# First cross attention of a four-layer block: where the heads are divided, and when TensorE weighs the values

## The chip, the cores and the metric

The program runs on one core of a Trainium2 chip. A core has five engines with an instruction queue each: TensorE (PE in the profile; PEld are its weight loads), VectorE (DVE), ScalarE (ACT), GpSimd (POOL) and SyncE (SP), which here only issues DMAs. They meet at semaphores alone. The metric is the device time of one execution in microseconds.

## What is computed

Four layers follow each other on `x` of 4 batches by 512 rows by 256: a cross attention, an expert attention, a second cross attention and product-key experts. The change is in the first, in its hand-over to the second, and nowhere else:

```python
def _L0_xattn_ref(x, kv, mask, attn_bias, WQ_w, WQ_b, WK_w, WK_b, WV_w, WV_b, WO_w, WO_b):
    B, S, E, H = (2, 512, 256, 16)          # B is 4 here: it is read from x.shape
    DK = E // H
    Q, K, V = ...                           # (x @ W.T + b), 16 heads of 16
    T = jnp.einsum('bhqd,bhkd->bhqk', Q, K) / math.sqrt(DK)
    T = T + attn_bias[:, None, :, :]
    T = jnp.where(m2[:, None, :, :] == 0, -1000000000.0, T)
    A = jax.nn.softmax(T, axis=-1)
    out = jnp.einsum('bhqk,bhkd->bhqd', A, V)
    out = out.transpose(0, 2, 1, 3).reshape(b, sq, E)
    return out @ WO_w.T + WO_b

x = x + tanh(g_xattn[0]) * _L0_xattn_ref(_layernorm(x), ctx_1024, mask, bias, ...)
```

## The kernel before

`a_attention` does the first attention in 64 steps: 4 batches, in each 4 groups of 4 heads, in each 4 tiles of 128 query rows. Step n has batch b = n // 16 and i = n % 16. All five queues are written out by hand, and each engine has a loop over n of its own. Everything is float32. The PSUM banks are SB (four, the scores of a step), TB (two, transposed probabilities), OB (the weighted values of a group) and MB (one, shared by all other jobs).

In step n TensorE does, in this order: `scores(n)` into SB, after VectorE has read the scores of step n-1; `turn_probs(n-1, 0)`, which transposes the probabilities of two of the four heads into TB, after both halves of step n-2 have been copied out of TB; at most one *job* in MB; `turn_probs(n-1, 1)` for the other two heads, into the same TB, after ScalarE has copied the first two out; and `weigh`, half of the value product of a pair of steps, two to three steps late. The jobs are the projections q, k and v (`queries`, `keys`, `values`), the transposes of the next batch's x (`turn_x`), the output projection of the last batch (`outputs`, one tile each) and `inverses`. Where a step has no job, `keep_busy` does one 128x512 matmul that nobody reads, once MB's last job has been taken. `slot(n)` is the table of jobs, and OUT_AT lists the steps of `outputs`. A job may start when the job before it has been taken out of MB (`bank_free`).

VectorE does `lowest` four times in step n: it adds the bias to the scores of a head and takes the least value. Then `take_pair(n-1)` copies TB's second half of step n-1 to SBUF, and then come what jobs it has to take (q, k, `update` of x by an output) and the statistics `stat` of the next batch. ScalarE does `take_pair(n-1)` of the first half, four exponentials (`spread_probs`, each with a row sum read from an accumulator), the jobs v and x, and once in four steps `take_o`, which copies OB to SBUF.

The value tile `vtok` has for each head 16 columns of values and 16 of ones, so that the 32 rows that a head has in OB are 16 of unnormalised output and 16 equal rows of the sum of its probabilities. Before, these sums are not read: VectorE takes reciprocals of the accumulated row sums (`invert`), TensorE spreads them over rows with 16 matmuls (`inverses`), and VectorE multiplies OB's copy by them (`normalise`) into `onorm`. `compact` on SyncE then moves the four heads of a group with four DMAs into `whole`, where a batch's 256 rows lie densely in two tiles, and `outputs` reads `whole`. The last batch's output projection is done within the second layer (`late_output` in `b_attention`), and the move of its last group too.

SyncE's queue also has `move`: eight DMAs each that spread q or k of two groups over strips of 32 partitions, which `scores` read; and `load_bias`. GpSimd has in batch b: `find_root`, `stage_x`, `shift_x` (layer norm of the next batch), `fold_bias` four times (mask and bias of the next batch into `bneg`, which `lowest` reads) and `fold_rows`.

## Time and profile before

| | us |
|---|---|
| median of 3 runs | 2248.33 |
| lowest and highest run | 2246.73, 2257.74 |
| the profiled execution | 2246.41 |
| its span, first to last instruction | 2244.6 |

| the first attention, in the profiled execution | us |
|---|---|
| scores of step 0 start | 19.18 |
| scores of step 16, 32 and 48 start | 101.48, 179.53, 257.58 |
| scores of step 63 start | 328.45 |
| TensorE's first matmul of the second layer | 346.83 |

Of the span, 347 us belong to the first attention, and the change touches nothing behind the first 100 us after it. A row of the timeline below is start, duration, engine, line, operation, out<-in and count; a matmul's own end is modelled and lies some 0.07 us behind the start of the next matmul that follows without a gap, so costs on TensorE are read from start to start. A float32 matmul is recorded as two instructions, a transpose as one.

### The profile page before, as it was taken

What the parts mean: (1) busy time and instruction counts of PE and PEld (TensorE: products, weight loads), DVE (VectorE), ACT (ScalarE), POOL (GpSimd) and SP (SyncE); (2) the same over time, 40 slices, a digit from 0 to 9 for tenths busy, and PEclk for the clock granted to TensorE, in tenths of its full rate; (3) what the DMA queues carried; (4) which work ended last, traced back from release to release, by engine and by line L of the source; (5) the groups of instructions that cost most, each with busy time, mean ns of one, the idle gap of its engine ahead of it and who ended that gap; (6) DMA issues with size and microseconds to landing.
All of it is one profiled execution on the core that took longest, in us unless ns stands there. A gap on an engine that the chain in (4) does not pass through costs nothing. (4 is left out here: it accounts for less than half of the span.)

```text
span 2244.6 us, 45912 instructions
## 1 busy us (share of the span) xinstructions
PE 2172.1 (97%) x18243; PEld 1463.3 (65%) x18276; DVE 1685.6 (75%) x4495; ACT 815.4 (36%) x1943; POOL 178.5 (8%) x427
## 2 busy tenths in 40 slices
PE   7999999999999999998999999999889999999998
PEld 3555554445756756775555555556678989898997
DVE  7888885866566566535887787877698988888895
ACT  4888881311311311302654554545321121111210
POOL 5553201000000000000000000000000000000000
PEclk9999999999999999999999999999999999999999
DMA  5111103000000003001000000001200000000000
GB/s 178 27 39 47 26 10 153 1 1 1 1 1 1 1 0 113 1 1 50 2 1 1 1 1 1 1 1 58 95 1 2 1 11 2 1 11 1 2 11 11
DMA packets 24165, 48.65 MB, mean 22 GB/s; under 512 B 5008, under 2 KB 13456, under 8 KB 22928
## 3 DMA queue, kind: packets, MB, share of 16 engines
q1 hardware_dynamic: 23952, 45.71, 6.1%
q8 instruction: 146, 2.39, 0.4%
q14 instruction: 67, 0.55, 0.1%
HBM read 37.57 MB, written 2.10 MB: 18 GB/s over the span
## 5 line engine op out<-in xcount | busy, mean ns | idle before, releaser
L2286 PE MATMUL banks<-work,big 128*128 128x128 f32 x2048 | 252.7, 277 | 2.0 <-PEq L376 1.3
L2286 PEld LDWEIGHTS banks<-work,big 128*128 128x128 f32 x2048 | 246.2, 193 | 7.6 <-issue 3.2
L614 ACT ACTIVATE work<-banks,work 128x512 f32<-128x512 f32 x256 | 174.8, 687 | 203.9 <-DVE work L731 203.9
L1085 PE MATMUL banks<-big,work 128*128 128x256 f32 x1024 | 241.3, 379 | 3.6 <-issue 3.3
L1009 PE MATMUL banks<-big,work 128*128 128x512 f32 x512 | 228.4, 600 | 1.6 <-DMA big<-in_B_val 1.4
L2379 ACT ACTIVATE work<-banks 128x512 f32<-128x512 f32 x128 | 76.5, 598 | 408.6 <-PE banks L2286 405.3
L1085 PEld LDWEIGHTS banks<-big,work 128*128 128x128 f32 x1024 | 195.0, 190 | 33.9 <-issue 1.9
L1904 ACT ACTIVATE work<-work 128x512 f32<-128x512 f32 x256 | 181.0, 711 | 0.0
L1009 PEld LDWEIGHTS banks<-big,work 128*128 128x128 f32 x512 | 96.0, 191 | 116.0 <-issue 113.3
L731 DVE TENSOR_REDUCE work<-banks 128x2 f32<-128x1024 f32 x128 | 150.4, 1217 | 7.7 <-PE banks L470 7.7
L1307 DVE CUSTOM_DVE_ANT_0 work<-banks,work 128x512 f32<-128x512 f32 (+3 forms) x128 | 57.7, 488 | 121.5 <-PE banks L1025 109.2
L1276 DVE TENSOR_TENSOR work<-banks,work 128x512 f32<-128x512 f32 x128 | 88.1, 691 | 65.7 <-PE banks L1009 65.4
L1808 PEld LDWEIGHTS banks<-ident,work 64*128 64x128 f32 x2048 | 75.5, 139 | 90.2 <-ACT work L1904 58.7
L1192 ACT ACTIVATE work<-work 128x512 f32<-128x512 f32 (+3 forms) x128 | 70.8, 554 | 168.7 <-DVE work L1307 168.6
L484 PEld LDWEIGHTS banks<-ident,work 64*128 64x128 f32 x2048 | 74.0, 139 | 89.1 <-issue 51.5
L2313 PE MATMUL banks<-big,wab 128*128 128x256 f32 x512 | 125.3, 388 | 3.5 <-DVE wab L2524 3.5
L470 PE MATMUL banks<-work 64*128 64x256 f32 x1024 | 124.6, 383 | 0.9 <-DVE work L724 0.9
L2313 PE MATMUL banks<-big,work 128*128 128x256 f32 x512 | 123.7, 387 | 0.8 <-DVE work L2524 0.8
L497 PE MATMUL banks<-big,wc 128*64 128x512 f32 x512 | 116.9, 598 | 5.2 <-ACT wc L635 2.9
L749 DVE COPY big<-banks 128x512 f32<-128x512 f32 x128 | 87.6, 684 | 38.9 <-PE banks L484 38.7
L740 DVE TENSOR_SCALAR work<-work 128x512 f32<-128x512 f32 x256 | 113.0, 484 | 4.5
L2303 PEld LDWEIGHTS banks<-wc 128*128 128x128 bf16 x3072 | 106.6, 98 | 13.3 <-issue 5.1
(248 smaller groups left out, 3791.7 us busy)
## 6 DMA issues: line engine op xcount, KB each, us to landing
work<-work SPq DMA_DIRECT2D x152, 32.0 KB, 2.0
big<-in_bias SPq DMA_DIRECT2D x16, 256.0 KB, 4.6
big<-in_B_val SPq DMA_DIRECT2D x8, 512.0 KB, 7.0
big<-in_B_out SPq DMA_DIRECT2D x1, 4096.0 KB, 18.9
big<-in_D_downT SPq DMA_DIRECT2D x4, 1024.0 KB, 5.5
big<-in_D_up SPq DMA_DIRECT2D x1, 4096.0 KB, 15.4
wc<-in_ctxT SPq DMA_DIRECT2D x1, 2048.0 KB, 7.8
wab<-in_L_ffn_w_q SPq DMA_DIRECT2D x1, 2048.0 KB, 10.1
```

The source lines that it names most:

```text
L470: last = eng.matmul(SB[i][:, j, c * 256:(c + 1) * 256], qT[r, t % 2, qt * P:(qt + 1) * P], kT[r, t % 2, c * 256:(c + 1) * 256], start=True ...
L497: last = eng.matmul(FB[0][j * DK:(j + 1) * DK, :], vtok[:, kt, h * DK:(h + 1) * DK], pT[:, (t % 2 * PAIR + j) * QT + kt, :], start=(kt == ...
L614: eng.activation(prob[:, n % NS * PAIR + j, :], SB[n % 2][:, j, :], ACT.Exp, bias=low[:, n % NS, j:j + 1], accum_out=rowsum[:, n % NS, j:j ...
L731: eng.tensor_reduce(low[:, n % NS, :], SB[n % 2], AX.X, ALU.max, negate=True).then_inc(low_ready.sem, 1)
L740: last = eng.tensor_scalar(one, one, rinv[:, n % NS, j:j + 1], None, ALU.mult)
L1009: last = eng.matmul(value_bank(b, n), xnT[:, kc, t * P:(t + 1) * P], w_val[:, kc, h * EB * DK:(h + 1) * EB * DK], start=(kc == 0), stop=(k ...
L1085: last = eng.matmul(XO[qt // 2][:, qt % 2 * D:(qt % 2 + 1) * D], spread[:, c % NG, qt * P:(qt + 1) * P], w_out[:, c, :], start=False, stop ...
L1276: eng.tensor_tensor(scaled[:, n % NG, :].rearrange("p (k e) -> p k e", e=EB), value_bank(b, n).rearrange("p (k e) -> p k e", e=EB), gm[:, ...
L1904: eng.activation(one, one, ACT.Exp, bias=low[:, n % 2, j:j + 1], scale=-1.0, accum_out=rowsum[:, n // QT % 2, at:at + 1]).then_inc(p_ready, 1)
L2286: last = eng.matmul(HP[n % 2][:, q * P:(q + 1) * P], down[:, (n * NJ + q) * KC + kc, :], xnT[par][:, kc, :], start=(kc == 0), stop=(kc == ...
L2303: last = eng.matmul(dst, hot[:, c, at, :], lot[c][:, at, f, :], start=(f == 0), stop=(f == 2))
L2313: last = eng.matmul(UPP[par][:, 0:D], G[par][:, j, :], up[:, j, :], start=(j == 0), stop=(j == ELO - 1))
```

## The change

- **Division.** `invert`, `inverses`, `normalise` and the row sums of the exponentials go. `take_o` copies OB, heads and sums, into one of two tiles. `gather_heads` on SyncE replaces `compact`: four DMAs move the rows of sums of a group into `sums`, four more the undivided heads into `whole`. `weigh_heads` on GpSimd then, for each *pair* of groups (one dense tile of 128 rows), finds 1/sums with a seed and three Newton steps and multiplies the tile: 11 instructions of 128x512. There are eight pairs; pair 2b and 2b+1 are the halves of batch b. `sums` is one tile, so a gather of the next pair waits until the pair before has been weighed (`weighted`). `outputs` waits for `weighted` instead of the moves.
- **Where GpSimd weighs.** Pair 2b-2 after the bias of batch b has been folded, pair 2b-3 ahead of `find_root(b)`, the last pair in the second layer.
- **Order on TensorE.** `weigh` stands between the two halves of `turn_probs`, behind the job, and no longer after the second.
- **Padding.** The unread matmuls of the steps without a job go. The loops end one step sooner.
- **Jobs** move: k to i = 2 and 4, v to 6, outputs to 8, 9, 12 and 15, x to 10 and 11.

```diff
-    OUT_AT = (5, 6, 10, 12)
+    OUT_AT = (8, 9, 12, 15)
...
+def gather_heads(eng, m, heads, whole, sums, g):
+    A = A_
+    for j in range(A.group):
+        r, at = (g % 2 * A.group + j) * A.dk, A.strip * j + A.dk
+        eng.dma_start(sums[r:r + A.dk, :], heads[at:at + A.dk, :]).then_inc(m["A.sums_moved"][g % 2], 16)
+    for j in range(A.group):
+        r, at = (g % 2 * A.group + j) * A.dk, A.strip * j
+        eng.dma_start(whole[r:r + A.dk, g // 2, :], heads[at:at + A.dk, :]).then_inc(m["A.compacted"][g], 16)
...
+def weigh_heads(eng, m, pair, whole, sums, inverse, product, step):
...
+    eng.tensor_scalar(inverse.bitcast(I32), sums.bitcast(I32), -1.0, INVERSE_SEED, ALU.mult, ALU.add).then_inc(step, 1)
+    for k in range(NEWTON):
...
+        eng.tensor_tensor(product, inverse, sums, ALU.mult).then_inc(step, 1)
...
+        eng.tensor_scalar(product, product, -1.0, 2.0, ALU.mult, ALU.add).then_inc(step, 1)
...
+        eng.tensor_tensor(inverse, inverse, product, ALU.mult).then_inc(step, 1)
...
+    eng.tensor_tensor(whole[:, kc, :], whole[:, kc, :], inverse, ALU.mult).then_inc(m["A.weighted"], 1)
...
+                def gather(b, g):
+                    eng.wait_ge(o_taken, G * b + g + 1)
                     if b >= 2:
                         eng.wait_ge(job_made, MADE[("out", b - 2, QT - 1)])
+                    eng.wait_ge(weighted, (G * b + g) // 2)
+                    gather_heads(eng, m, oT[g % 2], whole[b % 2], sums, g)
...
                 for b in range(1, B):
+                    if b >= 2:
+                        eng.wait_ge(row_step, ROWS * (b + 1))
+                        weigh_heads(eng, m, 2 * b - 3, whole[b % 2], sums, mm, bt, m["A.newton_step"])
                     find_root(eng, b)
                     stage_x(b)
...
+                    eng.wait_ge(fold_step, fold_at(b, QT - 1))
+                    weigh_heads(eng, m, 2 * b - 2, whole[(b - 1) % 2], sums, mm, bt, m["A.newton_step"])
...
                     if t == 0:
-                        for g in range(G):
-                            eng.wait_ge(compacted[g], 16 * GH * (b + 1))
+                        eng.wait_ge(weighted, 2 * b + 2)
...
-                    if 5 < n <= LAST and slot(n) is None:
-                        sem_, count = took([slot(k) for k in range(n) if slot(k) is not None][-1])
-                        eng.wait_ge(sem_, count)
-                        keep_busy(MB, 1)
+                    if n >= 3 and (n - 3) // 2 < LAST // 2:
+                        weigh((n - 3) // 2, (n - 3) % 2)
                     if 1 <= n <= LAST:
                         turn_probs(n - 1, 1)
-                    if n >= 3 and (n - 3) // 2 < LAST // 2:
-                        weigh((n - 3) // 2, (n - 3) % 2)
...
-                    eng.activation(one, one, ACT.Exp, bias=low[:, n % 2, j:j + 1], scale=-1.0,
-                                   accum_out=rowsum[:, n // QT % 2, at:at + 1]).then_inc(p_ready, 1)
+                    eng.activation(one, one, ACT.Exp, bias=low[:, n % 2, j:j + 1], scale=-1.0).then_inc(p_ready, 1)
```

How the queues change at two places. TensorE's queue in batch 1, steps i = 6 and 7, before: scores (L1794), a half of the transposes (L1808), the job (L1774 is `outputs`, L1762 `inverses`), the other half, `weigh` (L1824).

```order
L1794 MATMUL banks<-work 128x512 x4
L1808 MATMUL banks<-ident,work 128x64 x16
L1774 MATMUL banks<-wab,big 128x256 x2
L1808 MATMUL banks<-ident,work 128x64 x16
L1824 MATMUL banks<-wc,big 32x256 x8
L1794 MATMUL banks<-work 128x512 x4
L1808 MATMUL banks<-ident,work 128x64 x16
L1762 MATMUL banks<-ident,work 32x128 x16
L1808 MATMUL banks<-ident,work 128x64 x16
L1824 MATMUL banks<-wc,big 32x256 x8
```

The same steps of the changed kernel, where L1782 is `values`, L1852 `weigh`, L1836 the halves and L1822 the scores:

```order
L1822 MATMUL banks<-work 128x512 x4
L1836 MATMUL banks<-ident,work 128x64 x16
L1782 MATMUL banks<-wab,big 128x256 x4
L1852 MATMUL banks<-wc,big 32x256 x8
L1836 MATMUL banks<-ident,work 128x64 x16
L1822 MATMUL banks<-work 128x512 x4
L1836 MATMUL banks<-ident,work 128x64 x16
L1852 MATMUL banks<-wc,big 32x256 x8
L1836 MATMUL banks<-ident,work 128x64 x16
```

The second half of the transposes is now the last thing ahead of the next scores, and between its end and the next first half only the scores are left.

SyncE's queue from batch 1's second half into batch 2, before: L1589 is `compact`, L1579 `move`, L1567 the bias loads.

```order
L1589 DMA work<-work 16x512 [waits A_dve_took]
L1589 DMA work<-work 16x512 x3
L1579 DMA work<-work 16x512 [waits A_scores_made,A_dve_took]
L1579 DMA work<-work 16x512 x7
L1579 DMA work<-work 16x512 [waits A_scores_made,A_dve_took]
L1579 DMA work<-work 16x512 x7
L1567 DMA big<-in_bias 128x512 [waits A_fold_step] x4
L1589 DMA work<-work 16x512 [waits A_dve_took]
L1589 DMA work<-work 16x512 x3
```

The same stretch of the changed kernel, where L1407 moves sums, L1410 heads and L1609 is `move`:

```order
L1407 DMA work<-big 16x512 [waits A_heads_weighted,A_o_taken]
L1407 DMA work<-big 16x512 x3
L1410 DMA work<-big 16x512 x4
L1609 DMA work<-work 16x512 [waits A_scores_made,A_dve_took]
L1609 DMA work<-work 16x512 x7
L1609 DMA work<-work 16x512 [waits A_scores_made,A_dve_took]
L1609 DMA work<-work 16x512 x7
L1597 DMA big<-in_bias 128x512 [waits A_fold_step] x4
L1407 DMA work<-work 16x512 [waits A_heads_weighted,A_o_taken]
L1407 DMA work<-work 16x512 x3
L1410 DMA work<-work 16x512 x4
```

A gather has twice the DMAs, and its first one waits for GpSimd; the two moves of q and k stand behind it in the same queue.

## Rows read from the trace of the kernel before

**Rows 1.** Batch 2: length; PE, PEld, DVE, ACT, POOL busy; granted clock; DMA share.

```profile
179.50:257.60 78.10, 75.46 (x1087) 42.80 (x1083) 68.90 (x170) 65.33 (x153) 32.26 (x42) 1.00 0.14 36
```

**Rows 2.** Timeline of one step in batch 2, TensorE from its first scores to the next.

```profile
209.91 1.14 PE L1794 MATMUL banks<-work 16*128 16x512 f32 x8
...
212.90 0.71 PE L1808 MATMUL banks<-ident,work 64*128 64x64 f32 x16
...
213.55 1.07 PE L1824 MATMUL banks<-wc,big 128*32 128x256 f32 x16
...
214.55 1.14 PE L1794 MATMUL banks<-work 16*128 16x512 f32 x8
```

**Rows 3.** Timeline, steps 2 and 3, where nothing stands behind the second half.

```profile
32.71 1.14 PE L1794 MATMUL banks<-work 16*128 16x512 f32 x8
32.82 1.23 DVE L2003 COPY wc<-banks 128x1024 f32<-128x1024 f32 x1 [0.51 <-PE banks L1808]
...
34.19 0.71 PE L1808 MATMUL banks<-ident,work 64*128 64x64 f32 x16 [0.34 <-ACT work L1904]
...
39.04 0.71 PE L1808 MATMUL banks<-ident,work 64*128 64x64 f32 x16
40.96 1.12 PE L1808 MATMUL banks<-ident,work 64*128 64x64 f32 x16 [1.21 <-ACT wc L1896]
```

**Rows 4.** Timeline, a step with the job v, and the second half behind it.

```profile
201.70 1.99 PE L1742 MATMUL banks<-wab,big 128*128 128x256 f32 x8
...
203.63 0.71 PE L1808 MATMUL banks<-ident,work 64*128 64x64 f32 x16
```

**Rows 5.** Timeline of VectorE: it takes k, then statistics, then the next scores.

```profile
112.27 0.74 DVE L1967 SCALAR_TENSOR_TENSOR work<-banks,cols,work 128x512 f32<-128x512 f32 x1
...
113.53 0.69 DVE L1981 CUSTOM_DVE_ANT_0 work<-banks,work 128x512 f32<-128x512 f32 x1
```

**Rows 6.** Timeline of GpSimd in batch 2: start of the root, then the first fold of the bias.

```profile
205.76 0.20 POOL L1543 TENSOR_SCALAR work<-work 128x4 int32<-128x4 int32 x1 [22.30 <-DVE work L1945]
...
217.15 1.57 POOL L1530 TENSOR_SCALAR work<-work 128x512 f32<-128x512 f32 x1
218.81 1.28 POOL L1532 TENSOR_TENSOR work<-big,work 128x512 f32<-128x512 f32 x1
...
222.43 1.56 POOL L1530 TENSOR_SCALAR work<-work 128x512 f32<-128x512 f32 x1 [0.26 <-DVE work L1981]
```

**Rows 7.** Timeline of SyncE's queue: moves of q and k, bias loads.

```profile
107.77 10.21 SPq L1579 DMA_DIRECT2D work<-work  x16
118.02 2.00 SPq L1567 DMA_DIRECT2D big<-in_bias  x4
...
263.88 11.01 SPq L1579 DMA_DIRECT2D work<-work  x16
```

**Rows 8.** The page's DMA issues: median from issue to landing.

```profile
work<-work SPq DMA_DIRECT2D x152, 32.0 KB, 2.0
```

**Rows 9.** Timeline from the end of the first attention into the second layer.

```profile
343.39 1.08 PE L1762 MATMUL banks<-ident,work 128*32 128x128 f32 x32
344.40 1.98 PE L1781 MATMUL banks<-wab,ident 128*128 128x512 f32 x4
346.64 2.41 SPq L887 DMA_DIRECT2D work<-work  x4
...
353.23 3.78 PE L1009 MATMUL banks<-big,work 128*128 128x512 f32 x4 [1.41 <-DMA big<-in_B_val]
...
445.71 1.13 PE L989 MATMUL banks<-wab,work 128*128 128x256 f32 x4
```

**Rows 10.** One microsecond of step 3: length; PE busy; granted clock; DMA share.

```profile
41.00:42.00 1.00, 1.00 (x16) 0.50 0.29 66
```

**Rows 11.** Timeline of VectorE at the start: one operation, alone and beside GpSimd.

```profile
8.65 0.16 DVE L1548 TENSOR_TENSOR work<-work 128x4 f32<-128x4 f32 x1
...
9.56 0.47 DVE L1548 TENSOR_TENSOR work<-work 128x4 f32<-128x4 f32 x1
```

More of the change, by code:

```diff
@@ L982, in late_output @@
                     if t == 0:
-                        for g in range(A_.groups):
-                            eng.wait_ge(m["A.compacted"][g], 16 * A_.group * B)
+                        eng.wait_ge(m["A.weighted"], 2 * B)
                         eng.wait_ge(val_scaled.sem, val_scaled.at(0, VU))
@@ L1440, in slot @@
         more = b + 1 < B
[L1441 to L1443 removed]
+        if i in (0, 2) and b < B:
             return ("q" if i == 0 else "k", b, 1)
@@ L1754, in constant @@
                     last.then_inc(job_made, 1)
-                def inverses(g):
-                    eng.wait_ge(rinv_ready, g + 1)
-                    bank_free(eng, ("mult", g))
-                    for qt in range(QT):
-                        for j in range(GH):
-                            last = eng.matmul(MB[STRIP * j:STRIP * (j + 1), qt * P:(qt + 1) * P],
-                                              rinv[:, g % 2, qt * GH + j:qt * GH + j + 1].to_broadcast([P, STRIP]),
-                                              ident[:, :], start=True, stop=True)
-                    last.then_inc(job_made, 1)
                 def outputs(b, t, bank):
@@ L1838, in _ @@
                 queries(0, 0, MB)
-                for n in range(LAST + 4):
+                for n in range(LAST + 3):
                     b, i = divmod(n, PER)
@@ L1918, in _ @@
                     take_values(0, c, TB[:, c, :])
-                for n in range(LAST + 4):
+                for n in range(LAST + 3):
                     b, i = divmod(n, PER)
@@ L2036, in _ @@
                 take_first(("qg",), qs[:, 0, :], SB[3], 10, 1)
-                for n in range(LAST + 4):
+                for n in range(LAST + 3):
                     b, i = divmod(n, PER)
```

132 lines of the change are left out of this document (61 added, 71 removed).

## The prediction

> **What bounds the kernel now.** I read the busy times by stretch first, then single steps on the timeline. In batch 2 TensorE is busy 75.5 of 78.1 us at the full granted clock, 1.00, which is 2.4 GHz; VectorE is busy 68.9 and GpSimd 32.3 [rows 1]. So the first attention looks bound by TensorE. But a busy TensorE can be filled: the timeline of a step tells what ends each part. A step without a long job lasts 209.91 to 214.55, 4.64 us; the second half of the transposes takes 0.65, `weigh` 1.00 [rows 2]. Between the starts of the two halves lie 1.92 us even where no job stands there: in step 3 the row of the second half shows 1.21 us idle until ScalarE's copy [rows 3]. That leaves 4.64 - 1.92 - 0.65 - 1.00 = 1.07 for the scores. So the place between the halves is a gap of 1.3 us that unread matmuls or `inverses` fill for nothing, and only a longer job lengthens a step: v takes 1.93 [rows 4], giving 5.28. Six steps of 5.28 and ten of 4.64 are the 78.1 of a batch.
>
> **What the change seems to give, and the wait that it adds.** With `weigh` in that gap a step without a job would need 1.07 + 1.92 + 0.65 = 3.64. But `weigh` had cover to give as well. A first half may write TB only when VectorE has copied the last second half out. Before, that copy ran beside `weigh` and the scores; now only the scores stand between. Steps 2 and 3 show that order already, since there is no `weigh` yet: scores start at 32.71, the copy at 32.82 and lasts 1.23, and the first half starts at 34.19, 1.48 after the scores and 0.14 after the copy's end [rows 3]. (The row names ScalarE, whose last operation was nearer; the half needs only the second of its four exponentials.) So 1.07 becomes 1.48 in every step that TensorE bounds. The lengths of the new steps are then:
> no job 1.48 + 1.92 + 0.65 = 4.05; an output job (four records, half of v's eight, 0.97) 1.48 + 0.65 + 0.97 + 1.00 + 0.65 = 4.75; x, four single transposes, estimated at 0.5 from the same rate, 4.28; q, k, v 1.48 + 0.65 + 1.93 + 1.00 + 0.65 = 5.71. Steps with q, k or v get *longer*, by 0.43.
>
> VectorE ends some steps itself. From the start of scores: 0.11 to the copy, 1.14 until the next operation, 1.26 to take k or q and do one tile's statistics [rows 5], four `lowest` of 0.69 that overlap slightly, 2.6 in all: 5.1. That holds for i = 1 and 3, and 4.6 for i = 5, where the statistics are over. In the step after such a one the copy starts as early as the scores, and 0.25 is won back: 5.46 for i = 2, 4, 6.
>
> **A middle batch**: three of 5.71, three of 5.46, two of 5.10, one of 4.60, one of 4.05, four of 4.75, two of 4.28: 17.1 + 16.4 + 10.2 + 4.6 + 4.05 + 19.0 + 8.6 = 79.9 against 78.1. Taking the padding off TensorE saves nothing here.
>
> **The ring of SyncE and GpSimd.** A gather waits until the pair before has been weighed, and the moves of q and k wait behind it in SyncE's queue; GpSimd waits for the sums. One turn of it is one batch: gather of eight DMAs 5.1, move of q 5.1, move of k 5.1 (16 take 10.21 [rows 7]), bias 2.0, four DMAs of sums 1.9 and 2.0 to landing [rows 7, 8], weighing, root with staging and shift 11.4, four folds of 5.3 and weighing again. A weighing isn't in the trace. Its Newton step is a two-input operation, one with two constants and a two-input one with a wait each, the same trio that runs from 218.81 to 222.43, 3.6 [rows 6]; I take 3.5 for the shorter last wait. The seed lies between that trio's constant one (3.6 less two of 1.28, 1.0 with its waits) and the 1.57 of the form with a per-row operand; I take 1.6. With 1.3 for the product: 1.6 + 3 x 3.5 + 1.3 = 13.4, bounds 12.7 and 14.1. The ring: 15.3 + 2.0 + 3.9 + 13.4 + 11.4 + 21.2 + 13.4 = 80.6 at most, some 80 where a gather needn't wait its whole turn. It is level with TensorE's 79.9. I take 80.1, +2.0 a batch, +4.0 for two; bounds +1.5 and +6 a batch.
>
> The Trainium skill (GPSIMD Engine Reference, section Engine selection) says that elementwise work belongs to VectorE, GpSimd taking about twice as long with two inputs. Rows 6 show 1.28 for such an operation, and by that rule the division would better have stayed. The sum above would change only by its return to VectorE, some 0.9 us a group, and VectorE already ends three steps a batch; so the rule weighs against the ring, not for the old place.
>
> **First batch.** No outputs: steps 4 to 15 add up to 56.1 against 57.6, and the first steps, unpadded in both, gain about 0.5: -2.0. **Last batch** up to step 63: no k, q, v, x for another batch. 5.71 + 5.46 for its two jobs, two of 4.5 behind them (5.1 without statistics), 3.8 after those, three of 4.05, the output steps and those after them 9.5 + 4.2 + 3.8 + 4.75 + 4.2, and 4.7 where VectorE does the next layer's statistics: 67.3 against 70.87. Its first output at i = 8 waits for pair 5: k is taken 17.6 after the batch's start, moved by 22.8, sums landed by 26.7, weighed by 40.1, while TensorE is there at 38.2: 1.9 lost. -1.7. **The end**: `inverses` and the padding behind it, 343.39 to 346.3 [rows 9], go, 2.9; the last copies come later behind VectorE's statistics, 0.8 back: -2.1. **The second layer** starts with a gather of eight DMAs where four took 2.41, and the loads of its value weights queue behind; TensorE already waits 1.41 for the first [rows 9]: +2.5. The last pair's weighing is 13 us beside it, and its reader comes 99 us later, at 445.71 [rows 9]: hidden by far.
>
> **Sum**: -2.0 + 4.0 - 1.7 - 2.1 + 2.5 = +0.7, on the profiled execution's 2246.4: 2247.1. The median of the runs before is 1.9 above that execution, so I expect **2249**.
>
> **Rivals.**
> *The copy is hidden after all* (ScalarE, as the row names it, released those halves): then 1.07 stays, and the some 45 steps that TensorE bounds are 0.41 shorter, -18; the ring would cap it, a batch not below 80 for b = 1 and 2. That leaves the first and last batch: -8 to -11, 2239. Against it is the constant 0.14 behind the copy. Chance 0.10; if the ring is shorter as well, 2231.
> *The ring binds* and the kernel is slower. It decides from 80 us a turn, where it stands now. 16 moves also took 11.01 [rows 7], 0.05 more each, and 28 of them are in a turn: +1.5. GpSimd's 59 us a turn at 10% more: +6. Both together are +7.5 for each of two batches and +2 for the last: 2249 + 15 = 2264; half of it 2256. The page's queue shows the moves at either speed; GpSimd's rows are steady. Chance 0.20, of it 0.13 above the bound for slower.
> *The clock falls.* In step 3 waits of 0.4 and 1.2 follow each other, and the granted clock is 0.50, 1.2 GHz, for the next 3 us [rows 10]. The new steps i = 1 and 3 have waits of 0.4, 0.3 and 1.05 in 5.1 us. Each fall would cost about 1.5 of TensorE's work, at six places 9 us: 2258. Against it: denser steps lie between. Chance 0.08.
> *GpSimd holds up VectorE in the second layer.* At the start an operation of 0.16 took 0.47 beside GpSimd's [rows 11]. There the last weighing now runs beside VectorE's gate steps, each of which could wait for one of 1.28; eight of them 5 us, of which TensorE, with matmuls to do, feels 0 to 3: 2251. The Trainium skill (SBUF — State Buffer, Who interferes with whom) says that a VectorE operation with two SBUF inputs and a GpSimd one that reads SBUF block each other whole; rows 11 agree. Chance 0.05.
> That the change doesn't do what it says is out: the queues show `weigh` between the halves and no padding.
>
> **How the numbers follow.** The forecast has 0.57, its own range 2243 to 2255. A measurement tells 0.5% from no change, 11.2 us: below 2237.1 faster, above 2259.6 slower. Faster 0.08 (half of the first rival, the edge of the forecast); slower 0.17 (0.13 of the ring, the rest of clock and ring together); same 0.75. With a tenth left out on each side the range is 2238 to 2262.
>
> **What would show it.** First halves start 1.45 to 1.5 after their scores, TensorE's idle time ahead of them named as VectorE's copy; q, k, v steps 5.7, those without a job 4.05; scores of step 32 to 48 in about 80. GpSimd's weighing 13.4, SyncE's queue without long idle stretches ahead of the k move. First value matmul of the second layer some 2.5 us later after the gate. Wrong would be steps of 3.7, a batch of 85, or a granted clock below 1.00 in the middle.

## The result, and where the time went

In 15 runs of each, taken together, the changed kernel has a median of 2259.7 us (2254.66 to 2266.13) against 2251.0: the ratio is **1.0043**, 95% interval 1.0031 to 1.0054. It is slower, by a little less than the 0.5% that the forecast set as its bound. The time forecast, 2249, was 10.7 too low; 2259.7 still lies in the range of 2238 to 2262, at its upper end. Two runs of the kernel before (2496 and 6568 us), and one in a later set, were slow ones and count in no ratio; a ratio is taken over single runs, and so isn't quite the quotient of the medians. The profiled execution took 2254.66, its span is 2252.9. TensorE is less busy than before and the kernel takes longer (page, busy times; before it was 97%):

```profile
PE 2152.4 (96%) x17707; PEld 1451.6 (64%) x17740; DVE 1673.5 (74%) x4463; ACT 791.2 (35%) x1687; POOL 269.3 (12%) x515
```

Batch 2, from its first scores to the next batch's, by the same columns as [rows 1]:

```profile
180.43:260.73 80.30, 72.32 (x956) 39.88 (x953) 65.00 (x161) 59.49 (x89) 55.06 (x65) 1.00 0.16 41
```

TensorE is busy 3.1 us less in a batch (`inverses` is gone), and the batch became 2.2 longer. The timeline shows one step without a job, 55, and the start of step 56, in the order as the change makes it (L1822 scores, L1836 halves, L1852 `weigh`, L1802 an output job, L2010 VectorE's copy of the second half), and against [rows 2] and [rows 3] what it waits for:

```profile
292.71 1.14 PE L1822 MATMUL banks<-work 16*128 16x512 f32 x8
292.81 1.23 DVE L2010 COPY wc<-banks 128x1024 f32<-128x1024 f32 x1 [0.38 <-PE banks L1836]
294.19 0.72 PE L1836 MATMUL banks<-ident,work 64*128 64x64 f32 x16 [0.34 <-DVE wc L2010]
295.10 1.07 PE L1852 MATMUL banks<-wc,big 128*32 128x256 f32 x16 [0.20 <-ACT big L1931]
296.11 0.71 PE L1836 MATMUL banks<-ident,work 64*128 64x64 f32 x16
296.75 1.14 PE L1822 MATMUL banks<-work 16*128 16x512 f32 x8
298.23 0.71 PE L1836 MATMUL banks<-ident,work 64*128 64x64 f32 x16 [0.34 <-DVE wc L2010]
301.20 1.95 PE L1802 MATMUL banks<-wab,big 128*128 128x256 f32 x4 [2.26 <-POOL big L1433]
```

The first half starts 1.48 behind the scores and now the row names VectorE's copy; step 55 lasts 4.04. The last row is in step 56, the first output job of the last batch: TensorE waits 2.26 for GpSimd's weighing, and the job takes 1.95 where the others take 1.1. The rows by two microseconds (columns as in [rows 1]) show the granted clock at 0.50, 1.2 GHz, behind that wait:

```profile
300.00:302.00 2.00, 0.80 (x2) 0.74 (x3) 0.52 (x2) 2.00 (x5) 1.06 (x1) 0.83 0.00 0
302.00:304.00 2.00, 2.00 (x15) 0.80 (x18) 0.00 (x0) 0.45 (x1) 0.00 (x0) 0.50 0.19 41
```

GpSimd's weighing ahead of it, from the seed to the product, 288.82 to 301.06, is 12.2:

```profile
288.82 0.62 POOL L1422 TENSOR_SCALAR work<-work 128x512 int32<-128x512 int32 x1 [20.95 <-DMA work<-work]
289.53 1.28 POOL L1425 TENSOR_TENSOR work<-work 128x512 f32<-128x512 f32 x1
...
292.95 1.27 POOL L1425 TENSOR_TENSOR work<-work 128x512 f32<-128x512 f32 x1
...
299.79 1.27 POOL L1433 TENSOR_TENSOR big<-big,work 128x512 f32<-128x512 f32 x1
```

And the start of the second layer, where [rows 9] had one gather of 2.41 and a wait of 1.41:

```profile
348.35 2.40 SPq L1407 DMA_DIRECT2D work<-work  x4
350.80 2.48 SPq L1410 DMA_DIRECT2D work<-work  x4
...
353.33 5.14 SPq L889 DMA_DIRECT2D big<-in_B_val  x8
...
357.34 3.78 PE L1008 MATMUL banks<-big,work 128*128 128x512 f32 x4 [3.60 <-DMA big<-in_B_val]
```

Set side by side, the two profiled executions differ by 8.3 us of span, and the starts of the scores and of the layers say where (after minus before; "foreseen" is the prediction's term):

| stretch | foreseen | measured |
|---|---|---|
| up to the first scores (19.18 and 19.97) | 0 | +0.8 |
| batch 0 (82.30 and 78.99) | -2.0 | -3.3 |
| batches 1 and 2 (156.10 and 161.77) | +4.0 | +5.7 |
| batch 3 to its last scores (70.87 and 71.33) | -1.7 | +0.5 |
| from there to the first matmul of layer 2 | -2.1 | -1.9 |
| from there to its first value matmul (6.4 and 8.85) | +2.5 | +2.4 |
| from there to the late output (445.71 and 450.15) | 0 | +0.3 |
| the rest, whose code is the same | 0 | +3.8 |

The last row is two steps of 1.7, near 800 and 1030 us, where one execution has the clock at 0.50 for a while and the other has not. The twelve other profiles below are longer than before's there too, by 2 to 7, and the code is the same: it belongs to the executions, and the profile of before is a short one (2246.4, with a median of 2251.0). The fifteen runs of the changed kernel spread over 11.5 us and nearly order themselves by mean granted clock, 0.993 (2254.7) to 0.986 (2266.1); those of before in the sets below lie at 0.990 to 0.995. The profile of the changed kernel is of its fastest run, and so is the second one below: where the slower runs lose up to 11 us more, no trace shows.

### The profile page after: what moved, and what is told of

Same layout as the page of the kernel before. It is cut to its first block and busy times, and to the rows that moved or that the text cites. A ratio compares the mean times of both kernels' runs of the same rounds, so it can differ in the third digit from the quotient of the medians.

```text
span 2252.9 us, 44630 instructions
## 1 busy us (share of the span) xinstructions
PE 2152.4 (96%) x17707; PEld 1451.6 (64%) x17740; DVE 1673.5 (74%) x4463; ACT 791.2 (35%) x1687; POOL 269.3 (12%) x515
## 5 line engine op out<-in xcount | busy, mean ns | idle before, releaser
L1924 ACT ACTIVATE work<-work 128x512 f32<-128x512 f32 x256 | 164.4, 711 | 0.0
L1836 PEld LDWEIGHTS banks<-ident,work 64*128 64x128 f32 x2048 | 76.3, 139 | 102.9 <-ACT work L1924 58.3
L2010 DVE COPY wc<-banks 128x1024 f32<-128x1024 f32 x64 | 78.3, 1224 | 56.1 <-PE banks L1836 56.0
```

The costliest lines, as they stand in the source:

```text
L1924: eng.activation(one, one, ACT.Exp, bias=low[:, n % 2, j:j + 1], scale=-1.0).then_inc(p_ready, 1)
```

## The experiments

Each set is timed against the kernel before on the same chip; its median was 2248.7 in the first set (the changed kernel again, `weigh_back`, `no_newton`, `split_after`), 2248.0 in the second (`order_only`, `pad_end`, `bval_first`, `split_old`), 2250.3 in the third (the other four). Medians of different sets are compared through that kernel. Diffs are against the changed kernel or the kernel before, as the text says.

**The changed kernel again (`after_again`).**

> The changed kernel itself, in the company of the three others. Its runs so far lie between 2254.7 and 2266.1 us, with a mean granted clock of 0.993 to 0.986, and the longer ones are those of the lower clock. Theory (the clock is a matter of the execution, not of the kernel's plan alone): the same spread again, median about 2259, ratio to the kernel before 1.003 to 1.005, and in the profile half-clock stretches at other places than in the first. Rival (the fall follows the stall at the first output of the last batch): the half clock stands again right behind step 56.

2257.4 (2254.35 to 2263.28), ratio 1.0047 (1.0032 to 1.0062). Both theories are half right. The half clock stands behind step 56 again, from 301 to 305. But the second profile has one more, from 192 to 196, where the first has none. Its rows:

```profile
189.98 1.14 PE L1822 MATMUL banks<-work 16*128 16x512 f32 x8 [0.98 <-DVE work L2001]
...
191.85 3.63 PE L1769 MATMUL banks<-big,wab 128*128 128x512 f32 x4
```

This is step 34, i = 2, right behind the wait for VectorE that ends i = 1. Job k takes 3.63 where 1.9 is its time at full clock.

**`weigh` behind the second half again, the division left on GpSimd (`weigh_back`).** Against the changed kernel:

```diff
-                    if n >= 3 and (n - 3) // 2 < LAST // 2:
-                        weigh((n - 3) // 2, (n - 3) % 2)
                     if 1 <= n <= LAST:
                         turn_probs(n - 1, 1)
+                    if n >= 3 and (n - 3) // 2 < LAST // 2:
+                        weigh((n - 3) // 2, (n - 3) % 2)
```

> One part of the change undone: the two matmul groups of weigh stand behind the second half of the transposes again; the division stays on GpSimd and the jobs in their new places. Theory (VectorE's copy of the second half releases TB, and weigh was its cover): first halves start 1.07 after their scores again, steps without a job, with an output job and with x last 4.64, those with q, k or v 5.28, batch 2 lasts 78.1 if GpSimd's turn allows it and about 79 if not. First batch +1.5 to +2 against the changed kernel, middle batches -1 to -1.5 each, last batch +2 to +3 (its steps of 4.05 become 4.64): sum +0 to +2, 2259 to 2262. Rival (ScalarE's copy, as the row of before named it, sets the start of the first half): first halves stay at 1.48, steps without a job take 5.05, a batch 81 or more, the kernel 2270.

2278.4 (2264.2 to 2286.3), ratio 1.0128 (1.0102 to 1.0154), mean clock 0.976 to 0.989. The step model held: first halves at 1.07, steps 4.64 and 5.28. So `weigh` was the cover of VectorE's copy, as the prediction argued. The time was missed by 17, for a reason that neither theory had. Steps 8 and 9 on the timeline, their second halves and the `weigh` of step 9, with the clock by two microseconds:

```profile
66.97 0.71 PE L1836 MATMUL banks<-ident,work 64*128 64x64 f32 x16 [1.21 <-ACT wc L1918]
...
71.61 0.85 PE L1836 MATMUL banks<-ident,work 64*128 64x64 f32 x16 [1.21 <-ACT wc L1918]
72.39 1.93 PE L1852 MATMUL banks<-wc,big 128*32 128x256 f32 x16
```

```profile
70.00:72.00 2.00, 0.79 (x26) 0.68 (x24) 2.00 (x7) 1.55 (x3) 1.92 (x2) 1.00 0.24 57
72.00:74.00 2.00, 2.00 (x27) 0.87 (x23) 1.59 (x3) 1.92 (x4) 1.82 (x3) 0.51 0.01 2
74.00:76.00 2.00, 2.00 (x12) 0.52 (x8) 0.00 (x0) 0.00 (x0) 1.80 (x2) 0.50 0.00 0
```

The gap between the halves, 1.2 us without anything to do, comes in step after step here, and the clock goes to 0.50, for 10 us and again from 300 to 315 and from 324 to 339. It does so in batches 0 and 3, where steps without a job follow each other. In batches 1 and 2 the same gap stands in the steps i = 1, 3, 5 and 7, each between two steps with a job, and those eight kept the full clock. The kernel before had unread matmuls in those gaps. The next two runs put them back or take them off.

**The same, with the unread matmuls put back (`weigh_back_pad`).**

```diff
+                    if 5 < n <= LAST and slot(n) is None:
+                        sem_, count = took([slot(k) for k in range(n) if slot(k) is not None][-1])
+                        eng.wait_ge(sem_, count)
+                        keep_busy(MB, 1)
                     if 1 <= n <= LAST:
                         turn_probs(n - 1, 1)
```

> The changed kernel with weigh behind the second half again, and with the unread matmul of the kernel before between the halves of every step that has no job: the division on GpSimd and the new places of the jobs alone. Theory (what slowed the version without the unread matmuls by 30 us was the clock: 1.3 us of idle between the halves in steps without a job brought it to 0.50 seven times in the first attention): no half clock in the first attention behind its start, steps 4.64 and 5.28, batch 1 in 78.1, one wait of 2 to 4 at the first output of batch 3 (step 40), the second layer's start +2.5: 2253 to 2256, ratio 1.002 to 1.004. Rival (the clock fell for another reason, GpSimd's or the DMAs' work): half-clock stretches remain, 2268 or more.

2253.3 (2251.52 to 2260.1), ratio 1.0021 (1.0012 to 1.0031): **some 25 us faster by matmuls that nobody reads** (3.0 above before instead of 29.8). The same stretch as above:

```profile
70.00:74.00 4.00, 3.85 (x50) 1.70 (x46) 3.39 (x9) 3.47 (x5) 3.74 (x4) 1.00 0.15 35
```

In the first attention the clock is at 0.50 only at its start and, in this profile, for 3 us behind one long wait, that of step 40:

```profile
225.47 2.04 PE L1802 MATMUL banks<-wab,work 128*128 128x256 f32 x4 [3.79 <-POOL work L1433]
```

Batch 1 lasts 78.06, that of before. This run is also the price of the division on GpSimd with the new places of the jobs: +3.0 at the median.

**The kernel before without its unread matmuls (`no_unread`).**

```diff
-                    if 5 < n <= LAST and slot(n) is None:
-                        sem_, count = took([slot(k) for k in range(n) if slot(k) is not None][-1])
-                        eng.wait_ge(sem_, count)
-                        keep_busy(MB, 1)
```

> The kernel before without its unread matmuls, nothing else changed. Only steps without a job lose one: 6, 10, 12 in the first batch, six of the last. Theory (an empty gap of 1.3 us lets the clock fall, above all where two such steps stand together): one to three half-clock stretches of 3 to 8 us in batches 0 and 3, which cost half their length: 2250 to 2256. Rival (unread matmuls are worth nothing where no more than two such steps follow each other): 2248, same as before.

2261.7 (2259.2 to 2269.15), ratio **1.0058** (1.0043 to 1.0073). That is more than the theory gave and more than the whole change costs, though only ten unread matmuls go. Step 56, which like 57 behind it has no job:

```profile
302.47 0.71 PE L1808 MATMUL banks<-ident,work 64*128 64x64 f32 x16
304.39 0.72 PE L1808 MATMUL banks<-ident,work 64*128 64x64 f32 x16 [1.21 <-ACT wc L1892]
305.04 1.92 PE L1824 MATMUL banks<-wc,big 128*32 128x256 f32 x16
```

```profile
304.00:306.00 2.00, 1.61 (x28) 1.14 (x32) 2.00 (x6) 2.00 (x6) 0.00 (x0) 0.78 0.21 49
306.00:308.00 2.00, 2.00 (x20) 0.59 (x12) 0.38 (x1) 1.06 (x4) 0.00 (x0) 0.50 0.00 0
```

It stays at 0.50 to 322, and there are two shorter falls, 275 to 281 (step 50, a single empty step) and 339 to 343; batch 3 lasts 10.8 longer to its last scores. The single empty steps 6, 10, 12 and 52 kept the full clock. The fall at the start is longer than in [rows 10], but it stands in steps 3 and 4, ahead of the first matmul that is missing, and so its 1.8 us are not the edit's. Filling the gap that I had called free is worth 11 us.

**The other part of the change alone (`order_only`):** before, with `weigh` between the halves and no unread matmuls; the division stays on VectorE.

```diff
-                    if 5 < n <= LAST and slot(n) is None:
...
-                        keep_busy(MB, 1)
+                    if n >= 3 and (n - 3) // 2 < LAST // 2:
+                        weigh((n - 3) // 2, (n - 3) % 2)
                     if 1 <= n <= LAST:
                         turn_probs(n - 1, 1)
-                    if n >= 3 and (n - 3) // 2 < LAST // 2:
-                        weigh((n - 3) // 2, (n - 3) % 2)
```

> The kernel before with the other part of the change alone: weigh between the halves, no unread matmul in the steps; the division stays on VectorE with its matmuls of the inverses. Theory: first halves 1.48 behind their scores, a step with inverses 1.48 + 0.65 + 1.01 + 1.00 + 0.65 = 4.79, q, k or v 5.71 (5.46 where VectorE ends the step before), output 4.75, x 4.28: a middle batch 80.5 against 78.1, first batch -1.1, last -1.6, end -0.5, no loss in the second layer: sum +1.6, 2250 to 2251, the ratio 1.0007. Rival (the loss of the change comes from this reordering, with falls of the clock that the unread matmuls kept away): 2256 or more.

2256.0 (2254.53 to 2260.37), ratio 1.0041 (1.0028 to 1.0054), at a clock of 0.992 to 0.994. The time is the rival's and the reason is not: behind step 4 the first attention has no half clock. Batches 1 and 2 take 81.0 each against 78.1, +5.8 of the 6.9 by which the first attention ends later. A step with inverses and its neighbour:

```profile
139.50 1.14 PE L1794 MATMUL banks<-work 16*128 16x512 f32 x8
140.99 0.71 PE L1808 MATMUL banks<-ident,work 64*128 64x64 f32 x16 [0.34 <-DVE wc L1999]
141.63 1.08 PE L1762 MATMUL banks<-ident,work 128*32 128x128 f32 x32
...
144.15 1.14 PE L1794 MATMUL banks<-work 16*128 16x512 f32 x8
```

First half at 1.48, 4.65 in all, as foreseen within 0.14. The theory had 80.5: of the q, k and v steps five take 5.69 and only one is shortened behind VectorE, to 5.35. In the first and the last batch, where I had foreseen -1.1 and -1.6, -0.1 (with a fall of the clock in step 4) and -0.4 came. So the reordering by itself costs 8.0 and the moved division with its jobs 3.0, and the whole change 8.7, less than the 11.0 of both. That would fit with the steps of 4.05 that a batch has once `inverses` is gone, but no run separates it.

**`weigh` cut in two, in the changed kernel (`split_after`).** Four matmuls between the halves, four behind the second. `weigh` takes `half` as an argument:

```diff
-                    for kt in (2 * part, 2 * part + 1):
+                    for kt in (2 * part + half,):
...
-                    last.then_inc(av_made, 1)
+                    if half:
+                        last.then_inc(av_made, 1)
...
+                        weigh((n - 3) // 2, (n - 3) % 2, 0)
                     if 1 <= n <= LAST:
                         turn_probs(n - 1, 1)
+                    if n >= 3 and (n - 3) // 2 < LAST // 2:
+                        weigh((n - 3) // 2, (n - 3) % 2, 1)
```

> The changed kernel with weigh cut in two: the four matmuls of its first key tile stay between the halves of the transposes, the four of the second go behind the second half. Theory (a gap of 1.3 between the halves is free and VectorE's copy needs 0.4 of cover behind the second half, so 0.5 of weigh is the right price for each): first halves start at 1.07, a step without a job lasts 1.07 + 1.92 + 0.65 + 0.50 = 4.14, with an output 4.34, with q, k or v 5.28; TensorE alone would give a batch of 76.3, but GpSimd's turn with a weighing of 12.3 is about 79, so batches 1 and 2 last 78.5 to 80 and the rest shows up as waits at the first output. Against the changed kernel -3 to -8: 2252 to 2256. Rival (the first half waits for ScalarE): first halves at 1.48, a step without a job 4.55, batches over 80, no gain or a loss.

2253.2 (2248.03 to 2256.69), ratio 1.0018 (1.0008 to 1.0027): 4.2 below the changed kernel of the same set. First halves are at 1.07, steps without a job take 4.21 (I had 4.14), q, k and v 5.41. Half of `weigh` is cover enough. Part of what TensorE gains it loses again at step 40: batches 1 and 2 last 77.6 and 81.3, the second with 2.7 of wait at its first output and the clock at half behind it. What it waits for there is taken up below.

**The weighing cut short (`no_newton`).** The nine Newton operations are left out, so the heads are multiplied by the seed of the inverse and most of the division is missing.

```diff
-    for k in range(NEWTON):
+    for k in range(0):
```

> The changed kernel without the nine Newton operations of each weighing: the heads are multiplied by the seed of the inverse alone, so most of the division is left out and the output is off by up to some 12%. A weighing on GpSimd falls from 12.3 to about 2. Theory (the waits at the first output jobs, 1.3 at step 24 and 2.3 at step 56, and the half clock behind the second, come from GpSimd's weighing being late): both waits go, the half clock behind step 56 with them, batch 1 lasts 80.0, and the gate operations of VectorE at the start of the second layer take 0.43 again instead of 0.7 to 1.4. Against the changed kernel -3.5 for the waits and -1.7 for the clock: 2254. If the turn of GpSimd also bound the middle batches, they stay at TensorE's 79.9, so no further gain. Rival (TensorE's own steps and the second layer make all of the loss): 2258 to 2260.

2256.1 (2251.9 to 2258.96), ratio 1.0036 (1.0023 to 1.0049): 1.3 below the changed kernel of the same set at the median, which the intervals don't tell apart, and 2.4 in the profile, where 5 was expected. The waits at the first outputs are gone (steps 24 and 56 take 4.83), and layer 2 begins 3.5 earlier than in the changed kernel. But the value weights still come late there (first value matmul 9.7 behind the layer's start), and the clock fell at step 36. So in the changed kernel GpSimd's lateness is the smaller part of the loss.

**What keeps the first output waiting.** The changed kernel's own trace answers, from the end of GpSimd's weighing of one pair to step 40's output job, which needs the next pair (GpSimd, SyncE's queue, VectorE's copy of k, then GpSimd and TensorE):

```profile
186.32 1.27 POOL L1433 TENSOR_TENSOR work<-work 128x512 f32<-128x512 f32 x1
187.67 3.05 SPq L1407 DMA_DIRECT2D work<-big  x4
...
193.35 10.73 SPq L1609 DMA_DIRECT2D work<-work  x16
197.90 0.74 DVE L1987 SCALAR_TENSOR_TENSOR work<-banks,cols,big 128x512 f32<-128x512 f32 x1
204.12 2.00 SPq L1597 DMA_DIRECT2D big<-in_bias  x4
206.22 2.41 SPq L1407 DMA_DIRECT2D work<-work  x4
...
211.03 0.62 POOL L1422 TENSOR_SCALAR work<-work 128x512 int32<-128x512 int32 x1 [20.23 <-DMA work<-work]
...
223.45 1.10 PE L1802 MATMUL banks<-wab,work 128*128 128x256 f32 x4
```

The gather starts as soon as GpSimd has weighed. The move of q, taken long before, stands behind it in the queue, and is issued by 198.3; k is taken at 198.64. From there moves, bias and sums follow each other, and GpSimd, idle for 20.23, starts when the sums have landed. Behind 223.30 it has no gap until it has weighed the next pair, 267.88, and the next gather starts at 267.96. So the turn from gather to gather is 80.3, and all of it is work of SyncE, of the DMAs or of GpSimd but the 0.3 for which it waited for TensorE's k. It is the ring of the prediction, level with TensorE's batch.

In the version with `weigh` cut in two TensorE alone would be done in some 77 a batch, and there the ring binds:

```profile
193.23 10.58 SPq L1609 DMA_DIRECT2D work<-work  x16
195.74 0.74 DVE L1990 SCALAR_TENSOR_TENSOR work<-banks,cols,big 128x512 f32<-128x512 f32 x1
```

k is taken at 196.48, while the move of q is still being issued, so nothing in the turn waits for TensorE. Its length from one weighing to the next of its kind is 79.8, and step 40 waits 2.7. In `weigh_back_pad` it is 81.6, with a wait of 3.8. In that one and in `pad_end` there are 4.3 and 4.1 from the end of the sums' issue to the seed's start, where the changed kernel has 2.4.

**One unread matmul in steps 1 and 3 of batches 1 to 3 (`pad_end`)**, in the changed kernel, where TensorE waits for VectorE.

```diff
+                    if i in (1, 3) and 5 < n < LAST:
+                        sem_, count = took([slot(k) for k in range(n) if slot(k) is not None][-1])
+                        eng.wait_ge(sem_, count)
+                        keep_busy(MB, 1)
```

> The changed kernel with one unread 128x512 matmul behind the second half in steps 1 and 3 of each batch, where TensorE waits 1.05 for VectorE. Theory (these waits, three in 5 us, let the clock fall in some executions, which spreads the times from 2254 to 2266): step lengths stay at 5.1, the times draw together at 2254 to 2257 with clocks of 0.991 to 0.993, median about 2255. Rival (the falls come from elsewhere, the second layer's start or the later layers): the spread stays 2254 to 2266, median 2258 to 2260; with an unread matmul of 0.9 on the path where the wait is shorter +1 to +2.

2256.6 (2255.49 to 2262.72, five runs), ratio 1.0038 (1.0025 to 1.0051). At the median it can't be told from the changed kernel (8.6 above before, against 8.7), and the one high run keeps the spread. In the profiles of the four kernels that have this wait unfilled (the changed kernel twice, `no_newton`, `bval_first`), four falls of the clock stand in batches 1 and 2 away from an output's wait: steps 18, 34, 34 and 36, each right behind the wait of 1.0 that ends i = 1 or 3 (the rows above are one). In this profile there is none at those steps, and the clock fell behind the output's wait of step 40 instead, from 224 to 239. That the filling keeps the falls away is not shown: the first profile of the changed kernel had none there either. And the filling has a price in batch 3, where the wait is short: steps 49 and 51 take 5.10 instead of 4.49 and 4.58.

**The second layer's loads ahead of the last gather (`bval_first`)**, in the changed kernel.

```diff
-                gather_heads(eng, m, m["A.last_heads"], late_whole, m["A.sums"], A_.groups - 1)
...
                 eng.dma_start(w_out, a["B.out"]).then_inc(out_loaded, 16)
+                gather_heads(eng, m, m["A.last_heads"], late_whole, m["A.sums"], A_.groups - 1)
```

> The changed kernel with the last group's gather (eight DMAs) issued behind the loads of the second layer's value and output weights on SyncE's queue instead of ahead of them. Theory (in_B_val queues behind the gather and TensorE waits for it, 3.6 us at the first value matmul against 1.4 in the kernel before): the loads are issued 5 us earlier, the first value matmul comes 2.5 to 4 us earlier against the first matmul of the layer, the last weighing comes later but its reader is some 90 us away. Median 2.5 to 4 below the changed kernel's, 2254 to 2256. Rival (the loads need their 7 to 8 us to land in any order, or the gate ops beside GpSimd set that start): no change, 2258 to 2260.

2255.0 (2246.92 to 2258.92), ratio 1.0020 (1.0006 to 1.0033), against 1.0043 and 1.0047 for the changed kernel. At the median it is 7.1 above before, against 8.7 and 8.8; the runs spread over 12 us and settle the size of the gain poorly. The profile has four falls of the clock in the first attention, but at its own place the wait is gone:

```profile
354.58 4.15 SPq L888 DMA_DIRECT2D big<-in_B_val  x8
...
358.77 2.64 SPq L1407 DMA_DIRECT2D work<-work  x4
...
359.51 3.35 PE L1008 MATMUL banks<-big,work 128*128 128x512 f32 x4
```

From the layer's first matmul to the first value matmul there are 4.8, against 8.85 in the changed kernel and 6.4 before, and TensorE no longer waits for the loads. So the queue was the whole of this term, 4.0 here, the 1.4 of before included.

**Both mends together (`split_after_bval`).** `weigh` cut in two and the loads first.

> The changed kernel with both mends: weigh cut in two (2253.2 alone), and the second layer's loads ahead of the last gather (2255.0 alone). Theory (the two gains lie at different places and add up): about 3 below the first, 2249 to 2251, about level with the kernel before, with the wait for GpSimd's weighing at steps 40 and 56 still there. Rival (the layer's start is not what the second mend gained, its median fell in with fewer falls of the clock): 2252 to 2254.

2247.1 (2243.91 to 2252.61), ratio 0.9991 (0.9982 to 1.0000), 3.2 below before: the gains added up and a little more, though this profile too waits 3.6 at step 40, with a turn of 80.8.

**A version that beats both: before, with `weigh` cut in two and no unread matmuls (`split_old`)**, the division left on VectorE.

> The kernel before with weigh cut in two, four matmuls between the halves and four behind the second half, and no unread matmuls in the steps; the division stays on VectorE. Theory (1.3 us between the halves are free and 0.5 of weigh is cover enough for VectorE's copy): first halves at 1.07, a step without a job 4.14, inverses 4.4 to 4.6, output 4.34, x 4.14, q, k or v 5.28: a middle batch 75.8 against 78.1, first batch -3.8, last -4.4, sum -8 to -13: 2236 to 2241. Rival (the idle 0.3 to 0.8 between the halves brings the clock down, as the 1.3 did where weigh was moved back without the unread matmuls): half-clock stretches in batches 0 and 3, 2245 to 2260.

2240.9 (2238.97 to 2245.67), ratio **0.9971** (0.9959 to 0.9982). First halves at 1.07, no half clock from the first scores to the last, although up to 0.64 us of a gap stays empty beside its half of `weigh`. Steps with q, k or v take 5.41, 0.14 more than before, since both the job and half of `weigh` now stand in the gap. Hence the last run (`split_tuned`), with `weigh` whole behind the second half there:

```diff
+                    full = slot(n) is not None and slot(n)[0] in ("q", "k", "v")
-                    if n >= 3 and (n - 3) // 2 < LAST // 2:
+                    if not full and n >= 3 and (n - 3) // 2 < LAST // 2:
                         weigh((n - 3) // 2, (n - 3) % 2, 0)
...
+                    if full and n >= 3 and (n - 3) // 2 < LAST // 2:
+                        weigh((n - 3) // 2, (n - 3) % 2, 0)
```

> The version of before with weigh cut in two (2240.9), but with weigh whole behind the second half in the steps whose job is q, k or v. There the job of 1.93 fills the gap alone, and cutting weigh had made these steps 5.41 instead of 5.27. Theory: they go back to 5.28, six in each middle batch, 17 or so in all, 0.14 each: -2 to -2.5, 2238.5 to 2239, ratio to before 0.9955 to 0.9965. Rival (0.14 is VectorE's or ScalarE's, which end those steps either way): 2241, no change against the version with weigh cut everywhere.

2239.2 (2238.29 to 2242.39), ratio **0.9957** (0.9945 to 0.9970). Those steps are back at 5.28. An output step of it, TensorE alone:

```profile
144.82 1.14 PE L1794 MATMUL banks<-work 16*128 16x512 f32 x8
145.90 0.72 PE L1808 MATMUL banks<-ident,work 64*128 64x64 f32 x16
146.54 1.13 PE L1774 MATMUL banks<-wab,big 128*128 128x256 f32 x4
147.60 0.64 PE L1824 MATMUL banks<-wc,big 128*32 128x256 f32 x8
148.17 0.71 PE L1808 MATMUL banks<-ident,work 64*128 64x64 f32 x16
148.82 0.64 PE L1824 MATMUL banks<-wc,big 128*32 128x256 f32 x8
149.38 1.14 PE L1794 MATMUL banks<-work 16*128 16x512 f32 x8
```

And its batch 2, 75.8 long, with TensorE busy for all but 0.1:

```profile
173.25:249.06 75.81, 75.70 (x1085) 41.83 (x1081) 68.58 (x170) 65.05 (x153) 32.23 (x42) 1.00 0.14 37
```

## Why the prediction was right or wrong

**The wait that `weigh` had covered: right.** 1.48 instead of 1.07, the row of after names VectorE, and with `weigh` or half of it back behind the second half 1.07 returns. The rival in which ScalarE sets that start is out: nothing that ScalarE does was changed between the runs at 1.07 and those at 1.48.

**The new steps: right within 0.12.** No job 4.04 (4.05), q, k, v 5.69 (5.71), VectorE's 5.10 and 5.19 (5.1) and 4.56 (4.6), behind those 5.34 to 5.44 (5.46). An output step takes 4.83 (4.75) and x 4.36 (4.28): the four records of a job take 1.06 and 0.58 rather than 0.97 and 0.5, so half of v's eight was too little. The kernel before had the row to read it from: its own output jobs have four records with a duration of 1.13 where v's eight have 1.99. TensorE's own length of a batch is 80.2 and not 79.9.

**The gap filled "for nothing": wrong, and the step that failed.** The prediction read from [rows 2] and [rows 3] that unread matmuls cost nothing, and concluded that taking them off changes nothing, so its sum has no term for the clock. They also gave something: 11 us in the kernel before, some 25 in the version with `weigh` behind. The changed kernel escapes most of this because `weigh` itself fills the gap. What it still loses by the clock is 1.7 behind step 56 (1.5 in the second profile), and a fall in step 18, 34 or 36 in some executions of it and its neighbours; how its slower runs lose more stays open. [rows 10] had shown it: an idle gap, and then 0.50. I had made it a rival at 0.08, with the right steps (i = 1 and 3) and about the right price for one fall (1.5, where a step with one is 1.6 longer), but with six of them. Of four profiles of kernels with these waits three have such a fall, one or two each.

**The ring: right in size, partly by luck, and it set less than I said.** The turn is 80.3 where 80.6 was summed. Two errors cancel: the two weighings take 12.3 each with their hand-over, not 13.4, and the part from the gather to the landed sums takes 23.1 without the wait for k, not 21.2. The queue was ready for k's move 0.3 ahead of k in batch 2, 0.4 in the last batch and earlier still in batch 1, so k, which TensorE makes, still led, and what counts is the path from k's copy over moves, bias and sums to the weighing. The prediction followed this path for the last batch and got a wait of 1.9 where 2.3 came; in the middle batches it left it out, and there it gave 1.2 at step 24, where the sums landed 4.1 behind their issue, and 0.1 at step 40. The rival in which the ring binds didn't come in the changed kernel. It came where TensorE was faster, with turns of 79.8 to 81.6 and waits of 2.7 to 3.8.

**GpSimd's weighing: too dear.** 12.2 against 13.4 and the lower bound of 12.7. A trio takes 3.42 (3.5), but the seed 0.7 from start to start, not 1.6. I had put it above the 1.0 of the constant form with its waits, towards the form with a per-row operand. It costs what the constant form costs: `L1427`, on floats, takes 0.62 as well.

**Second layer: right.** +2.4 for +2.5. The rival on VectorE beside GpSimd happened without a price. The gate operations of 128x256 (L1255, L1264) took 1.17 and 1.37 beside the weighing where they had taken 0.42 and 0.43, but they ended at 361.56 and TensorE had value matmuls to do. That the first of [rows 11] stood alone was a wrong reading: GpSimd was at work from 7.59 to 9.11, and the operation at 8.65 took 0.16 all the same, which the rule of the page named there doesn't explain; the one of 0.47, from 9.56, ended with GpSimd's of 9.39 to 10.02. The Trainium skill (SBUF — State Buffer, Who interferes with whom) says that a VectorE operation with two SBUF inputs contends with a GpSimd one that reads SBUF; the two reductions of the same chain, with one input, kept 0.42, so in this chain the trace agrees.

**Where the division belongs.** The Trainium skill (GPSIMD Engine Reference, Engine selection) sends elementwise work to VectorE. With the best order found on each side, GpSimd's version takes 2247.1 and VectorE's 2239.2. Part of this is the treatment of the q, k and v steps, which only VectorE's version got: with `weigh` cut in every step the two are 3.2 and 7.1 below before. The runs agree with the page, though not by the operation's own length alone: the weighing waits for sums that SyncE has to carry, and both its turns of 12.2 lie in the ring. How much each gives no run separates.

**The sum.** Foreseen +0.7 for the profile, measured +8.2: 1.7 in the middle batches, 2.2 in the last, 3.8 of clock in unchanged layers, 0.8 of start, 0.3 ahead of the late output, less 1.3 in the first batch (the half clock of [rows 10] did not come). The median is 5.0 above the profile, as the runs with a lower clock are many; I had put 1.9. Seen by medians, 8.0 of the 10.7 are the change (+8.7 for +0.7), and 2.7 are the kernel before, for which I had three runs with a median of 2248.3 where fifteen give 2251.0. The range reached up to 2262 to leave room for the ring and for six falls of the clock. Neither came as described, so that it held the result is in part luck.

## What to carry to other kernels

A matmul that nobody reads may hold the clock: before taking it off, look whether an idle gap of that length stands anywhere else in the trace and what the granted clock does behind it. An operation moved out of its place takes its cover with it, and the cheapest place is often half here and half there: here, with the division on VectorE, 0.5 of `weigh` between the halves and 0.5 behind gave 0.3%, and 0.4% with the steps left out that a job fills; all of it between the halves cost 0.4%, and all of it behind, without unread matmuls, 0.6%. When a long chain through several queues feeds one job, adding up a turn tells whether it can bind; follow it from event to event as well, since a single late link makes the job wait while the turn still has room.

## What the runs showed of the hardware

- Idle gaps of 1.2 us in steps of 4.64, one step behind the other, were followed by TensorE at 1.2 GHz (0.50) instead of 2.4, for 3 to 17 us. Alone between two filled steps, such a gap kept 1.00 in twelve cases (eight in `weigh_back`, in its batches 1 and 2, four in `no_unread`) and had a fall behind it in one (`no_unread`, step 50).
- A wait of 1.0 behind smaller ones had a fall behind it in some executions and not in others: four times in the batches 1 and 2 of four profiles.
- The same gap of 1.2 with one unread matmul in it: 1.00 from step 4 on, in the kernel before. With the 0.5 us of half a `weigh` in it: 1.00 from the first scores to the last (`split_old`, `split_tuned`).
- GpSimd's 128x512 operation with two constants takes 0.62, with integers or floats; with two inputs 1.27.
- GpSimd's first operation on the sums, which waits for their DMAs, started 2.4 to 4.3 us behind the end of their issue, from one execution to the next, in the same place of the program.
